# Fused graph-network kernel: in the second pair pass, half of the slab loads move from SyncE's queue to ScalarE's

## What is computed

```python
# x: (64, 128, 128); for each graph, all pairs (i, j) of nodes
d = abs(x[:, :, None, :] - x[:, None, :, :])      # (64, 128, 128, 128)
h = d @ W1.T + b1                                 # 64 hidden channels
h = (h - mean(h)) / sqrt(var(h) + EPS) * g1 + be1 # statistics over ALL graphs and pairs
h = leaky(h)
s = h @ W2.T + b2                                 # one score for each pair
A = softmax(where(A_init > 0, s, NEG))
y = (A @ x) @ Wg.T + bg                           # then batch norm, leaky, output projection
```

## Time and profile before

| | |
|---|---|
| three timed runs | 2121.3, 2126.96, 2137.3 us; median 2126.96 us |
| profiled execution, its own time | 2132.9 us |
| its span, first to last instruction | 2131.1 us |
| TensorE, VectorE, ScalarE, GpSimdE busy, share of the span | 82%, 82%, 65%, 28% |
| moved by the DMA queue that SyncE issues to, whole span | 283.37 MB |
| second pair pass | from 1675 to about 2080 us |

### The profile page before, as it was taken

How to read it: one execution, slowest core, us unless ns; L and a number is a source line. 1 busy time by engine, 2 the same in 40 slices (tenths; PEclk the granted TensorE clock), 3 DMA queues, 4 the chain that set the end, 5 groups by cost and what they waited for, 6 DMA issues and landing times. The chain is left out here.

```text
span 2131.1 us, 43841 instructions
## 1 busy us (share of the span) xinstructions
PE 1756.3 (82%) x13707; PEld 1115.9 (52%) x13707; DVE 1741.0 (82%) x2696; ACT 1387.3 (65%) x3197; POOL 600.1 (28%) x458
## 2 busy tenths in 40 slices
PE   2967777767766989996799999999999588888886
PEld 1855555656643666665565555555555244444445
DVE  5878888888775877776899999999999477777777
ACT  0533333333325998994388888888888587777774
POOL 1520000000003444544454444444544111111110
PEclk9978999898876998996599999999999899999998
DMA  6000000000000000000055555555555899999993
GB/s 178 0 5 1 1 0 0 0 0 0 0 1 14 4 6 6 6 5 20 33 221 223 225 217 226 219 224 223 220 223 220 312 344 342 341 343 343 339 329 86
DMA packets 123567, 292.98 MB, mean 137 GB/s; under 512 B 21376, under 2 KB 57608, under 8 KB 123288
## 3 DMA queue, kind: packets, MB, share of 16 engines
q1 hardware_dynamic: 106360, 283.37, 35.8%
q10 hardware_dynamic: 16896, 8.39, 1.4%
q0 software_dynamic: 256, 0.56, 0.1%
HBM read 150.45 MB, written 141.82 MB: 137 GB/s over the span
## 5 line engine op out<-in xcount | busy, mean ns | idle before, releaser
L1273 POOL TENSOR_TENSOR pair_ring<-hd 128x2048 f32 (+1 forms) x64 | 269.5, 4211 | 312.4 <-DVE pair_ring L1298 312.4
L1358 ACT ACTIVATE v_hid<-v_psW 128x1024 f32<-128x1024 f32 x256 | 263.6, 1030 | 87.1 <-PE v_psW L1396 87.1
L734 DVE TENSOR_REDUCE m_part<-m_psS 128x128 f32<-128x2048 f32 (+1 forms) x128 | 258.9, 2023 | 70.1 <-PE m_psS L601 70.1
L1294 DVE TENSOR_TENSOR pair_ring<-v_psX,hd 128x2048 f32<-128x2048 f32 x128 | 292.6, 2288 | 18.9 <-PE v_psW L1396 18.8
L1396 PE MATMUL v_psW<-pair_ring,p_w1T 128*64 128x512 f32 x1024 | 288.8, 597 | 0.0
L1361 ACT ACTIVATE v_junk<-v_psW 128x1024 bf16<-128x1024 f32 x256 | 263.4, 1029 | 0.0
L601 PE MATMUL m_psS<-m_onehot,m_tableT 32*128 32x128 f32 x3584 | 153.3, 310 | 127.2 <-DVE m_part L734 123.0
L1396 PE MATMUL v_psW<-pair_ring,l_w1T 128*64 128x512 f32 (+1 forms) x1024 | 252.5, 587 | 0.0
L1387 PE MATMUL v_psW<-p_ends,v_weights 128*64 128x512 bf16 x1536 | 235.3, 381 | 6.1 <-DMA v_fold<-in_c_fold_dram 6.1
L1544 DVE SCALAR_TENSOR_TENSOR pair_ring<-pair_ring 128x1024 f32<-128x1024 f32 x128 | 156.5, 1226 | 65.6 <-ACT pair_ring L1611 65.6
L601 PEld LDWEIGHTS m_psS<-m_onehot,m_tableT 32*128 32x128 f32 x3584 | 130.0, 209 | 146.6 <-issue 78.9
(11 more groups left out here) (255 smaller groups left out, 3392.6 us busy)
## 6 DMA issues: line engine op xcount, KB each, us to landing
pair_hidden<-v_hid SPq DMA_DIRECT2D x256, 512.0 KB, 2.6
pair_ring<-pair_hidden SPq DMA_DIRECT2D x128, 1024.0 KB, 7.2
adj_ring<-in_adj_dram ACTq DMA_DIRECT2D x16, 256.0 KB, 5.0
x_all<-in_x_dram ACTq DMA_DIRECT2D x16, 256.0 KB, 5.5
out_dram<-x_all SPq DMA_DIRECT2D x16, 256.0 KB, 2.3
pair_scores<-s_rot SPq DMA_DIRECT2D x64, 32.0 KB, 5.1
s_fwd<-pair_scores SPq DMA_DIRECT2D x64, 32.0 KB, 5.0
s_wide<-pair_scores SPq DMA_DIRECT2D x64, 32.0 KB, 5.5
```

What stands on the lines that cost most here:

```text
L734: nc.vector.tensor_reduce(part[:, i % 2, r, :], psS[:, :, 0:w].rearrange("z q (c i) -> z i q c", i=N), AX.XY, ALU.max).then_inc(reduced, 1)
L1273: nc.gpsimd.tensor_tensor(D[:, home(u, SLABS - 1), :].rearrange("c (h d i) -> c h d i", h=2, i=N), one, far, ALU.subtract).then_inc(psub_d ...
L1294: nc.vector.tensor_tensor(slab(s), own, windows(hd, n, s)[1], ALU.max).then_inc(max_done, 1)
L1358: nc.scalar.activation(hid[:, s, :], psW[:, buf, :], ACT.Identity, accum_out=hsum[:, bass.ds(m, 1)]).then_inc(evacuated, 1)
```

## The change

The even loads of graphs 2 to 63 are issued by ScalarE. Its step n, after its waits for the even load of graph n and for `p0_mm` of graph n-1, issues the even load of graph n+1 (the same load, after the same `p0_mm`, as SyncE did in its step n-1), and then runs `hid`. SyncE keeps the odd loads, which no longer stand behind the wait for `p0_mm`, and the three score DMAs. ScalarE's program is written straight out for all 71 steps instead of looped; the other engines keep their loops.

```diff
-def load_products(sp, ring, loaded, hidden, j):
-    sp.dma_start(ring[:, j % 4, :].rearrange("p (m c) -> p m c", m=2),
+def load_products(eng, ring, loaded, hidden, j):
+    eng.dma_start(ring[:, j % 4, :].rearrange("p (m c) -> p m c", m=2),
                  hidden[2 * j:2 * j + 2].rearrange("m p c -> p m c")).then_inc(loaded[j % 4], 16)
...
+        def at(step, n):
+            step(n, n % 2, n // 2, *(0 <= n - lag < B for lag in range(LAGS)))
+
+        def unrolled(step):
+            for n in range(B + LAGS - 1):
+                at(step, n)
...
             def _(sp):
-                def load(j):
-                    load_products(sp, ring, loaded, hidden, j)
...
                     if n + 2 < B:
-                        sp.wait_ge(p0_mm, done(n))
-                        load(2 * n + 4)
                         sp.wait_ge(affine_done, done(2 * n + 1))
-                        load(2 * n + 5)
+                        load_products(sp, ring, loaded, hidden, 2 * n + 5)
...
                     if zero:
                         act.wait_ge(loaded[slot(p, 0)], 16 * t + 16)
                         act.wait_ge(p0_mm, done(n - 1))
+                        if one and n + 1 < B:
+                            load_products(act, ring, loaded, hidden, 2 * n + 2)
                         nc.scalar.activation(hid[:, 0, :], h[:, slot(p, 0), 0, :], ACT.Relu, bias=beta[:, 0:1],
...
-                graphs(act, step)
+                unrolled(step)
```

More of the change, by code:

```diff
@@ L1449, in phase_pair_scores @@
         LAGS = 8
+        def at(step, n):
[3 more added lines that the diff above has]
+                at(step, n)
         def graphs(eng, step):
             def peeled(n):
-                step(n, n % 2, n // 2, *(0 <= n - lag < B for lag in range(LAGS)))
+                at(step, n)
             for n in range(8):
```

## The result

The changed kernel takes 2164.9 us, median of four runs (2157.4 to 2172.5), against 2127.0 (2121.3 to 2137.3): 1.0181 of before, with a 95% interval of 1.0143 to 1.0219. That is slower by 38 us, where 17 were forecast. The direction and the place were right, the size was not.

The account below looks back on a forecast made before the run. A loop through `second`, `rows`, affine, `hy`, attention matmul and `first` was taken to bound the steady step at 6.43 us, loads close behind. Terms 13.8 + 3 + 0 + 0 = +17 us gave about 2144 us, range 2114 to 2172.

Parts of the forecast that it names:

- What bounds the kernel: Steady steps: a loop between TensorE and ScalarE through `hy` makes 6.43 us a step, loads half a microsecond behind.
- The odd load now goes first and the even load, needed first, comes last: Steady steps: SyncE issues the odd load 1.7 us earlier, 1.3 us ahead of the even one.
- 2P = 4.85 + E: Step P if even landings bind; E runs from a pair's first issue to both landed; P 6.68 us, +13.8 us.
- The gate: ScalarE's queue: the next even load cannot be issued before the last even load has landed; no separate cost given.
- The first steps: Start of the pass, where loads bind: later even loads cost +3 us, from 0 to +5.
- ScalarE's issue: One load issue between `p0_mm` and `hid`: 0.45 us, covered by idle time before `rows`, cost 0.
- Straight code: ScalarE's unrolled program: register work saves at best 8 us, fetches cost 0 to +3; taken as 0.
- The score DMAs: SyncE's queue: behind one load instead of two, they can only come earlier; gain 0.
- The second queue brings no bandwidth: DMA engines: both queues run on the same 16 engines, so sharing doesn't shorten the sum of the work.
- Clearly slower: Rival, steady steps: E 9.1 or ScalarE's issue 0.7 us or more, late landings adding up; 2161 us, chance 0.22.
- Faster: Rival, steady steps: loads stretch the loop and ScalarE's loop code costs more than shown; 2109 us, chance 0.13.
- nothing changes: Rival, steady steps: E at 8.0 or less, step stays 6.43 us, only first steps count; 2130 us, chance 0.22.

Follow-up runs that it names:

- Run 7: Kernel before, with `hy` moved on ScalarE from between the two affines to just before `rows`; 0.9844, 2099.0 against 2133.4 us.
- run 2: Kernel before, one queue, SyncE issuing the odd load first and the even load second, after `p0_mm`; 1.0100, 2154.8 against 2133.6 us.
- run 6: Changed kernel, with ScalarE issuing the next even load ahead of its wait for the present one; even load first in one stretch, odd in another; 1.0075, 2150.4 us.
- run 3: Changed kernel, with ScalarE's load issue moved behind `hid`; 1.0138, 2162.5 us.
- run 10: Kernel before, one queue, odd load first, and SyncE's even load also waiting until the last even load has landed; 1.0153, 2163.6 us.
- run 1: Kernel before, with only ScalarE's program written straight out and all loads left with SyncE; 0.9992.
- run 8: Changed kernel, with both loads issued by ScalarE behind `hid`, even first, and only score DMAs left with SyncE; 1.0015.
- run 9: Kernel before, one queue, even load first, with SyncE also waiting for the last even load's landing before issuing the pair; 0.9999.

## Why the prediction was right or wrong, point by point

- **What bounds the kernel** was read rightly. Run 7 cut the loop through `hy` and the step fell by 0.5 us; no steady `hid` waited for a load, so there was nothing to gain from moving the loads alone.
- **The odd load now goes first and the even load, needed first, comes last.** Right, and shown by run 2 (order alone, 1.010) and by the two stretches of run 6.
- **The step that failed** is the sum 2P = 4.85 + E with E = 8.5: its term of 0.25 us a step measured 0.41, or 22.5 us instead of 13.8. The chain was right. In the late step shown above 4.8 us lay between the landing at 1873.87 and the odd issue at 1878.64. But E was 8.8 there (odd issue 1878.64, even landing 1880.00 + 7.4), and 8.8 in the mean of the 36 late landings from step 9 on; (4.85 + 8.8) / 2 = 6.8 is the measured step. E had been read from loads in the old order, issued together at `p0_mm`, and was put in as a constant. With the odd load first it is larger and gives way to the rest: 8.9 for the late landings of run 2, 9.3 in run 3, where the chain beside it was shorter. The prediction also said that one even load cannot be issued before the last has landed, and gave this no price. It has one: by the table under run 10 the order alone makes 22 us in the pass, and the gate on top of it 14 more, each from one execution. The gate is no simple chain of late loads, though. In the changed kernel's trace 35 even loads of steps 9 to 63 are issued right behind the last landing, but of 35 late landings only 18 are followed by another, since a load issued so late can land quickly (5.3 us in the lines above). Why E is 8.8 in one step and 7.8 in the next stays open.
- **The first steps** were sized at +3, at most +5, and measured +7.8 (53.6 against 45.8 us). The gate without a price accounts for most of the miss: the order alone made +3.9 in these steps, order and gate +7.5 (runs 2 and 10).
- **ScalarE's issue** was to be hidden in idle time. It takes 0.37 us, as SyncE's did. Where `hid` is late it lies on the path, since `rows` follows `hid` at once; the sum had it there, with 0.45. Run 3 moved the issue off that path and shows no gain. The queued issues of the earlier trace rows, with their 0.7 us and more, had rightly been set aside.
- **Straight code**: nothing, as taken (run 1). The page "Runtime: NRT & Kernel Launch" of the Trainium skill, section "Instruction fetch mechanics", gives fetch stalls at branches as a reason to unroll; in this loop unrolling brought 0.9992, no gain.
- **The score DMAs** came earlier, as taken: the one that writes scores landed after 4.2 us in the median instead of 5.2, and nothing in the steady part waited for them. In the first stretch of run 6 SyncE did, and that held the order right.
- **The second queue brings no bandwidth**: the DMA share fell, and with two queues and the even load first the kernel is as before (run 8; in the first stretch of run 6 the step was 6.37 us, with a slab load in each queue). This agrees with the section "Issuing engines are not separate DMA queues" of the page "DMA: Bandwidth & Descriptors" of the Trainium skill. That page's reason to do it at all, the sequencer's time, was not short here.
- **The rivals.** "Clearly slower" described the outcome, 2161 us against 2165, and named "every late landing delays the next issue too" as its reason. It was to decide from E = 8.8 on, which is what E measured; that its time fits so well is partly luck, since its step was 6.98 us (6.84 and 6.95 measured) and its first steps +4. I gave it 0.22 because a typical pair took 8.5 us; that measures the loads in the old order, not what a late landing does to the next. "Faster" and "nothing changes" have no run for them.

Open: the changed kernel (1.018 and 1.020) lies some 0.3 to 0.5% above run 10, with overlapping intervals, and the traces show no difference of the passes beyond that between two executions of the changed kernel. Whether the 0.37 us on ScalarE or the sharing of two queues has a small part of its own is not settled.

## What to carry to other kernels

Ask of two prefetches not only when each is issued but which lands first, and whether that is the one needed first; a transfer that was early enough can do harm by being earlier. And when an issue is moved to a computing engine, it inherits every wait ahead of it there. Put it before the waits that it doesn't need. A wait for the previous transfer of the same kind cost nothing here while the loads had time to spare (run 9), and 14 us of the pass once they had none (run 10 against run 2). And look for a falling DMA share in a step that waits for loads: here it said that the transfers were issued too late, not that they moved too slowly.

## What was not expected of the hardware

A DMA share of 0.97 at 341 GB/s left more room than it seemed: in run 7 the same traffic ran at 1.00 and 370 GB/s, with steps 7% shorter. And the same program can settle in either of two orders within one execution (run 6): 27 steps of 6.37 us, then, after two longer ones (8.2 and 7.1 us) that began with a wait of 3.1 us for a load, 23 steps of 6.76 us. And of a load issued with nothing under way, the first packet started 1.0 us after the issue and the full rate came 1.9 us after it (the changed kernel at 1878.64). In the kernel before, where the last odd load was still being moved, the engines moved 410 GB/s in that time.
